# Second batch's head: tile 4 modulated between the moments, all row sums on VectorE, squares behind the copies of the transposes

## The chip, the cores and the metric

One core of a Trainium2 chip runs the whole program: two transformer layers on two sequences of 512 rows of 512 values. The metric is the device time of one execution in microseconds (us), lower being better. The core has five engines which each run their own queue strictly in order and meet through semaphores: TensorE (PE in the rows; its weight loads are PEld), VectorE (DVE), ScalarE (ACT), GpSimd (POOL) and SyncE (SP), which issues transfers.

## The reference, cut to what matters

The change touches only the step between the second layer's attention and its last block, for the second sequence. There the reference computes, row by row (512 values in a row):

```
h = _layernorm(x) * (1 + cb) + sb              # per row: (x - mean) / sqrt(var + 1e-5), then scaled and shifted
x_norm = h * rsqrt(mean(h * h) + RMS_EPS)
H_res_logits  = (x_norm @ W_res.T).reshape(B, T, 4, 4) + H_res_base
H_pre_logits  = x_norm @ W_pre.T + H_pre_base
H_post_logits = x_norm @ W_post.T + H_post_base
H_res = sinkhorn_log(H_res_logits)             # 50 alternating normalisations of every row's 4x4 matrix
...
return x + gb * (x_mixed + y_distributed)
```

`cb` and `sb` depend on the sequence alone. The three logits are 24 numbers per row. The 50 Sinkhorn iterations need the 16 `H_res` logits of the rows, and the kernel runs them for all 1024 rows at once.

## The kernel before, in words

The rows are held in 8 tiles of 128 rows by 512 values; tiles 0 to 3 are the first sequence, 4 to 7 the second. `acc[:, i, :]` is tile i of x, `hh[i // 4][:, i % 4, :]` the same tile of h. Each stage of a tile is a method of one name in each engine's class (`Vector`, `Scalar`, `Tensor`, `Pool`, `Sync`), and the story function calls them in one order; an engine that has nothing to do in a stage skips it. So the order of the calls is the order of every engine's queue. Nothing is planned at run time: the order is written by hand, and a wait at the front of a queue holds everything behind it on that engine.

The stages of one tile i of a head, the lines being those of the profile:

- `moments`: VectorE takes statistics of the row (L1114, L1116) and makes the negative mean and the variance plus epsilon (L1118, L1119); GpSimd makes the reciprocal root (L1773) and its product with the mean (L1775).
- `norm`: ScalarE writes the normalised row to `hh` (L1491).
- `scaled_rows`: VectorE multiplies by 1 + cb (L1126, in place); sb is then added in place either by GpSimd (L1783) or, for tiles 5 and 7, by VectorE (L1130). `h_rows_at(i)` names the semaphore of whoever adds, and the readers of the finished rows wait for it.
- `square`: ScalarE sums the squares of the row (L1606: the activation and a read of its accumulator).
- `turn_l`: TensorE transposes the tile's four 128x128 blocks (L800), and ScalarE copies them from PSUM to `hT4` (L1614).
- `rms`: VectorE scales the sum of squares (L1244), after waiting for ScalarE's square of this tile, and GpSimd takes the power -1/2 (L1857).
- `logits`: TensorE multiplies `hT4` by the 24 columns (L811, eight instructions per tile), and VectorE scales the result by the reciprocal root and adds the bias (L1250), after waiting for both.

For the first sequence the head is interleaved with the attention (`head(E, 0)`). For the second it stands alone in `last_head`, since the attention's last group has to be finished first (`residual_last`, L1105 and L1107). Before the change its order is: moments and norm of tiles 4 to 7; scaled rows of 4 to 7; then per tile `square`, `turn_l`, `rms`, and the `logits` of the tile before. The three waits of VectorE that matter below are these:

```
ve.wait_ge(*a_n("h", i))          # scaled_rows: this tile's norm on ScalarE
ve.wait_ge(*a_ss(i))              # rms: this tile's sum of squares on ScalarE
ve.wait_ge(*p_lg("l", i))         # logits: this tile's product on TensorE
```

Behind the head VectorE starts the Sinkhorn chain (`sk_scale`, L1256, which waits for the logits of tile 7), a chain of small dependent operations of VectorE up to `H` (L1304); beside it the other engines make the branch of the block. Then `finish` mixes the streams and writes the eight output tiles.

Of the kernel before, what the change touches and what calls it, by code (L numbers as in the profile page):

```python
# [69 lines left out]
def build(nc, I, out, cst_w):  # L70
# [3 lines left out]
    def sig(name, step=1):  # L74
        return Sig(ctx.enter_context(nc.semaphore(name)), step)
# [150 lines left out]
    for b in range(2):  # L226
# [53 lines left out]
    v_fw, v_fT, v_res, v_ln, v_hl, v_ffn, v_aw, v_qkv, v_part, v_pt, v_nm, v_mx, v_out = [sig(n) for n in  # L280
        ("v_fw", "v_fT", "v_res", "v_ln", "v_hl", "v_ffn", "v_aw", "v_qkv", "v_part", "v_pt", "v_nm", "v_mx", "v_out")]
# [8 lines left out]
    g_x, g_ln, g_vp, g_rot, g_mix, g_rr, g_pre = [sig(n) for n in ("g_x", "g_ln", "g_vp", "g_rot", "g_mix", "g_rr", "g_pre")]  # L290
# [58 lines left out]

    def h_rows_at(i):  # L350

        return v_ln("h", "d", i) if i in (5, 7) else g_ln("h", i)

    def most(t):

# [116 lines left out]
    class Tensor(Stages):  # L472
# [322 lines left out]
        def turn_l(self, i, bk):  # L795
            pe = self.e
            pe.wait_ge(*h_rows_at(i))
            pe.wait_ge(*self.drain[bk])
            for k in range(4):
                mm = pe.transpose(banks[bk][:, k * 128:(k + 1) * 128], hh[i // 4][:, i % 4, k * 128:(k + 1) * 128], ident)  # L800
            mm.then_inc(*p_lg.up("T", i))
            self.drain[bk] = a_hc(i)
# [32 lines left out]
    class Vector(Stages):  # L835
# [285 lines left out]
        def scaled_rows(self, i):  # L1121
            ve, b = self.e, i // 4
            h_ = hh[b][:, i % 4, :]
            ve.wait_ge(*a_n("h", i))
            ve.wait_ge(*d_mt[4, b](1))
            ve.tensor_tensor(h_, h_, mt[1, 4, b][:, :], ALU.mult).then_inc(*v_ln.up("h", "c", i))  # L1126
            if i in (5, 7):
                ve.wait_ge(*v_ln("h", "c", i))
                ve.wait_ge(*d_mt[3, b](1))
                ve.tensor_tensor(h_, h_, mt[1, 3, b][:, :], ALU.add).then_inc(*v_ln.up("h", "d", i))  # L1130
# [210 lines left out]
    class Scalar(Stages):  # L1341
# [259 lines left out]
        def square(self, i):  # L1601
            ac = self.e
            ac.wait_ge(*h_rows_at(i))
            if i:
                ac.wait_ge(*a_ss(i - 1))
            ac.activation(junk[:, :], hh[i // 4][:, i % 4, :], ACTF.Square,  # L1606
                          accum_out=fs["ss"][:, i:i + 1]).then_inc(*a_ss.up(i))
# [70 lines left out]
    class Pool(Stages):  # L1678
# [96 lines left out]
            po.tensor_tensor(nmr[:, i:i + 1], nmean[:, i:i + 1], rs[:, i:i + 1], ALU.mult).then_inc(*g_rr.up(of, i))  # L1775

        def scaled_rows(self, i):
            if i in (5, 7):
                return
            po, b, h_ = self.e, i // 4, hh[i // 4][:, i % 4, :]  # L1780
            po.wait_ge(*v_ln("h", "c", i))
            po.wait_ge(*d_mt[3, b](1))
            po.tensor_tensor(h_, h_, mt[1, 3, b][:, :], ALU.add).then_inc(*g_ln.up("h", i))  # L1783
# [594 lines left out]

    def last_head(E):

        E.residual_last(1)
        for i in range(4, 8):
            E.moments("h", i), E.norm("h", i)
        for i in range(4, 8):
            E.scaled_rows(i)
        for i in range(4, 8):
            E.square(i)
            E.turn_l(i, E.spin())
            E.rms(i)
            if i > 4:  # L2390
                E.logits(i - 1, E.spin())
        E.logits(7, E.spin())

    class Sink:
# [207 lines left out]
    def story(E):  # L2602
        layer0_head(E)
        layer0_loop(E)
        middle(E)
        line = stream(E, pass_a_line)
        parts(E, 0, line)
        parts(E, 1, line)
        pending = joined(stream(E, head, 0), stream(E, mixes, 0))
        attentions(E, line, pending)  # L2610
        pending.rest()
        last_head(E)
        merged(stream(E, first_half), stream(E, branch, 0)).rest()
        merged(stream(E, second_half), stream(E, branch, 1)).rest()
        stream(E, finish).rest()
        E.end()
# [87 lines left out]
```

## Time and profile before

| what | us |
|---|---|
| median of 3 runs | 1483.64 |
| lowest, highest run | 1483.23, 1487.5 |
| the profiled execution's own time | 1483.97 |
| its span, first to last instruction | 1481.5 |
| VectorE busy in the span | 1007.2 (68%) |
| TensorE busy in the span | 1230.3 (83%) |
| ScalarE busy in the span | 622.5 (42%) |
| GpSimd busy in the span | 737.1 (50%) |

The shares are averages over very different stages. The stretch that the change touches is some 18 us long, from 1314.6 (the first statistics of tile 4) to 1332.2 (the first Sinkhorn operation), and it is read by itself. In a timeline each line is one instruction or some alike in a row: start in us from the span's start, duration in us, engine, line, operation, output and input tiles with their shapes, count; in brackets the idle time of the engine ahead of it and what ended it. The duration of a line with xN runs from the first one's start to the last one's end.

### The profile page before, as it was taken

How to read it: one execution, taken by the hardware profiler on the slowest of the kernel's cores; microseconds unless marked ns; L12 is line 12 of the kernel's file. 1: busy time of each engine (PE TensorE's matmuls, PEld its weight loads, DVE VectorE, ACT ScalarE, POOL GpSimd, SP SyncE). 2: the span in 40 equal slices, each digit the busy share in tenths (PEclk: the TensorE clock that was granted, in tenths of full speed). 3: DMA queues.
4: the chain of work that ended last, by engine and by line, in shares of the span. 5: the costliest groups of instructions: out<-in, count | busy, mean ns of one | idle time of the engine just before them, and what ended most of it. 6: DMA issues, size and time to landing. Idle time of an engine off the chain costs nothing. (4 is left out here: it accounts for less than half of the span.)

```text
span 1481.5 us, 18424 instructions
## 1 busy us (share of the span) xinstructions
PE 1230.3 (83%) x6008; PEld 867.2 (59%) x6008; DVE 1007.2 (68%) x1721; ACT 622.5 (42%) x1166; POOL 737.1 (50%) x740
## 2 busy tenths in 40 slices
PE   4889999999999999999999999988979988961100
PEld 2578767776776776876776777766743333430000
DVE  5845665656655656665666656597778898659898
ACT  2334333433433433433433343338327777753303
POOL 0465756656755675576665675698410012031107
PEclk9899999999999999999999999999969999975555
DMA  4211122123122212222212111140485310000001
GB/s 163 79 52 59 45 77 72 58 57 89 54 72 72 63 45 72 58 57 65 64 44 78 54 47 57 51 137 7 91 152 81 52 48 2 1 1 0 0 0 57
DMA packets 70487, 86.45 MB, mean 58 GB/s; under 512 B 6789, under 2 KB 40741, under 8 KB 69818
## 3 DMA queue, kind: packets, MB, share of 16 engines
q1 hardware_dynamic: 68138, 81.52, 20.2%
q10 hardware_dynamic: 2256, 3.77, 0.9%
q8 instruction: 49, 0.80, 0.2%
q14 instruction: 44, 0.36, 0.1%
HBM read 77.49 MB, written 7.51 MB: 57 GB/s over the span
## 5 line engine op out<-in xcount | busy, mean ns | idle before, releaser
L1695 POOL TENSOR_TENSOR sw<-sw,sinT 128x512 f32<-128x512 f32 x80 | 103.3, 1291 | 138.9 <-ACT sw L1425 138.9
L1474 ACT ACTIVATE yTh<-yF 128x512 fp32r<-128x512 f32 x64 | 40.4, 632 | 308.1 <-DVE yF L1043 308.1
L1208 DVE TENSOR_REDUCE nm<-banks 128x2 f32<-128x1024 f32 x128 | 151.3, 1219 | 26.0 <-PE banks L750 25.9
L1709 POOL TENSOR_TENSOR dec<-gb,gcol 128x512 f32<-128x512 f32 x64 | 70.3, 1099 | 190.7 <-DVE Sd L1009 187.6
L1587 ACT ACTIVATE Pb<-banks 128x512 f32<-128x512 f32 x256 | 135.0, 601 | 47.6 <-PE banks L771 47.2
L981 DVE SCALAR_TENSOR_TENSOR gs<-tg,banks 128x512 f32<-128x512 f32 x64 | 44.0, 688 | 117.6 <-ACT tg L1432 117.6
L547 PE MATMUL banks<-hTh,wgh 128*128 128x512 f32 x256 | 122.2, 477 | 0.0
L599 PE MATMUL banks<-st,qt 128*128 128x128 f32 x384 | 78.8, 288 | 37.8 <-DVE Sd L1009 21.1
L625 PE MATMUL banks<-woh,yTh 128*128 128x512 f32 x256 | 104.8, 410 | 2.7 <-ACT yTh L1474 2.7
L547 PE MATMUL banks<-hTh,wqh 128*128 128x512 f32 x256 | 106.3, 415 | 0.0
L547 PE MATMUL banks<-hTh,wgl 128*128 128x512 f32 x256 | 101.0, 394 | 0.0
L547 PE MATMUL banks<-hTl,wgh 128*128 128x512 f32 x256 | 100.7, 393 | 0.0
L547 PE MATMUL banks<-hTh,wql 128*128 128x512 f32 x256 | 100.7, 393 | 0.0
L625 PE MATMUL banks<-wol,yTh 128*128 128x512 f32 x256 | 100.5, 393 | 0.0
L547 PE MATMUL banks<-hTl,wqh 128*128 128x512 f32 x256 | 99.9, 390 | 0.0
L1049 DVE TENSOR_TENSOR yTl<-yF,yTh 128x512 fp32r<-128x512 f32 x64 | 69.8, 1091 | 41.5 <-ACT yTh L1474 41.2
L771 PE MATMUL banks<-qsT,ksT 50*128 50x512 f32 x256 | 90.2, 487 | 8.2 <-DVE hh L1232 6.1
L600 PE MATMUL banks<-xc,Sd 128*128 128x128 f32 x512 | 94.1, 282 | 0.3 <-DVE Sd L1009 0.3
L976 DVE TENSOR_TENSOR tt<-banks,cosT 128x512 f32<-128x512 f32 x80 | 55.3, 691 | 52.7 <-ACT sw L1425 51.9
L1700 POOL TENSOR_TENSOR qT<-tt,sw 128x512 f32<-128x512 f32 x64 | 83.9, 1310 | 14.6 <-DVE tt L976 6.5
L599 PEld LDWEIGHTS banks<-st,qt 128*128 128x128 f32 x384 | 63.3, 200 | 47.0 <-DVE Sd L1009 25.3
L1432 ACT ACTIVATE tg<-banks 128x512 f32<-128x512 f32 x64 | 38.3, 598 | 119.9 <-PE banks L547 119.9
(310 smaller groups left out, 3291.4 us busy)
## 6 DMA issues: line engine op xcount, KB each, us to landing
gb<-g_scr SPq DMA_DIRECT2D x64, 256.0 KB, 3.5
raw<-in_wmod SPq DMA_DIRECT2D x40, 256.0 KB, 2.7
raw<-in_wg SPq DMA_DIRECT2D x32, 256.0 KB, 2.7
raw<-in_wo SPq DMA_DIRECT2D x32, 256.0 KB, 2.9
raw<-in_wq SPq DMA_DIRECT2D x30, 256.0 KB, 2.7
qsT<-q_scr SPq DMA_DIRECT2D x22, 256.0 KB, 7.1
q_scr<-hl SPq DMA_DIRECT2D x28, 128.0 KB, 4.8
mt<-mods_scr SPq DMA_DIRECT2D x12, 256.0 KB, 4.5
```

The costliest lines, as they stand in the source:

```text
L547: mm = pe.matmul(banks[bk][:, :], w_[:, k, :], x_[:, k, b * 512:(b + 1) * 512], start=(c == 0), stop=(c == 11))
L599: pe.matmul(o, qt[:, h, :], st[:, h, :], start=True, stop=False)
L600: mm = pe.matmul(o, Sd[:, h, :], xc[:, h, :], start=(n == 0), stop=True)
L625: pe.matmul(banks[bO][:, :], yTh[:, h, :], w_[:, :], start=(h == 0 and n == 0), stop=False)
L771: pe.matmul(banks[bk], k_[64 * g:64 * g + 50, p // 4, kt * 128:(kt + 1) * 128], q_[64 * g:64 * g + 50, p % 8, :], start=True, stop=True).t ...
L976: ve.tensor_tensor(tt1[j][:, :], banks[bk][:, :], cosT[:, :], ALU.mult).then_inc(*v_cos.up(kind, t, n))
L1049: ve.tensor_tensor(yTl[:, :, :], yF[:, :, :], yTh[:, :, :].bitcast(F32), ALU.subtract).then_inc(*v_yl.up(s))
L1208: ve.tensor_reduce(nm[:, b, i, p:32:16], pairs[z_][:, :].rearrange("p (g t) -> p g t", g=2), AX.X, ALU.max, negate=True).then_inc(*v_nm.up ...
L1587: ac.activation(Pb[kt % 2][:, 2 * g + pr, :], banks[bk], ACTF.Exp, scale=0.25).then_inc(*a_exp.up(b, qd, kt, pr, g))
L1695: po.tensor_tensor(s_[:, :], s_[:, :], sinT[:, :], ALU.mult).then_inc(*g_rope.up("sin", kind, t, n))
L1700: po.tensor_tensor(dst, tt1[j][:, :], s_[:, :], ALU.add).then_inc(*g_rope.up("add", kind, t, n))
L1709: po.tensor_tensor(dec[:, :, :], gb[s % 2][:, :, :], bc(gcol[:, t % 2, heads(t), n], 2, 128), ALU.subtract).then_inc(*g_dec.up("sub", s))
```

## The change

Three edits. `h_rows_at` and the two `scaled_rows` make VectorE add sb for all four tiles of the second sequence (GpSimd adds for the first sequence alone). In `last_head` tile 4's scaled rows and its transposes with their copy come ahead of the moments and norm of tile 7. And the rest goes tile by tile: for tiles 5 to 7 the scaled rows, the transposes with their copy and the logits of the tile before, then the square and `rms`, so that a square stands behind the copy of its tile's transposes on ScalarE.

```
     def h_rows_at(i):
-        return v_ln("h", "d", i) if i in (5, 7) else g_ln("h", i)
+        return v_ln("h", "d", i) if i > 3 else g_ln("h", i)
...
-            if i in (5, 7):
+            if i > 3:
                 ve.wait_ge(*v_ln("h", "c", i))
                 ve.wait_ge(*d_mt[3, b](1))
                 ve.tensor_tensor(h_, h_, mt[1, 3, b][:, :], ALU.add).then_inc(*v_ln.up("h", "d", i))
...
         def scaled_rows(self, i):      # GpSimd
-            if i in (5, 7):
+            if i > 3:
                 return
...
     def last_head(E):
         E.residual_last(1)
+        for i in (4, 5, 6):
+            E.moments("h", i), E.norm("h", i)
+        E.scaled_rows(4)
+        E.turn_l(4, E.spin())
+        E.moments("h", 7), E.norm("h", 7)
         for i in range(4, 8):
-            E.moments("h", i), E.norm("h", i)
-        for i in range(4, 8):
-            E.scaled_rows(i)
-        for i in range(4, 8):
+            if i > 4:
+                E.scaled_rows(i)
+                E.turn_l(i, E.spin())
+                E.logits(i - 1, E.spin())
             E.square(i)
-            E.turn_l(i, E.spin())
             E.rms(i)
-            if i > 4:
-                E.logits(i - 1, E.spin())
         E.logits(7, E.spin())
```

## Rows read from the trace of the kernel before

**Rows 1.** Chain of waits that ended last: start us, duration us, what.
```profile
1319.51 0.69 DVE hh L1126
1320.22 1.27 POOL hh L1783
1321.53 1.97 PE banks L800 x8
```

**Rows 2.** Timeline of VectorE, from tile 4's statistics to Sinkhorn.
```profile
1314.63 0.69 DVE L1114 BATCH_NORM_STATS2 bst<-acc 128x6 f32<-128x512 f32 x1
...
1317.84 0.68 DVE L1114 BATCH_NORM_STATS2 bst<-acc 128x6 f32<-128x512 f32 x1
...
1318.85 0.14 DVE L1119 TENSOR_SCALAR ve<-mv 128x1 f32<-128x1 f32 x1
1318.91 1.28 DVE L1126 TENSOR_TENSOR hh<-hh,mt 128x512 f32<-128x512 f32 x2
1320.23 1.80 DVE L1130 TENSOR_TENSOR hh<-hh,mt 128x512 f32<-128x512 f32 x1
1321.95 1.28 DVE L1126 TENSOR_TENSOR hh<-hh,mt 128x512 f32<-128x512 f32 x2
...
1327.72 0.24 DVE L1250 SCALAR_TENSOR_TENSOR lg<-banks,r,rbc 128x24 f32<-128x24 f32 x1 [1.72 <-PE banks L811]
1327.88 0.14 DVE L1244 TENSOR_SCALAR ss<-ss 128x1 f32<-128x1 f32 x1
...
1331.88 0.24 DVE L1250 SCALAR_TENSOR_TENSOR lg<-banks,r,rbc 128x24 f32<-128x24 f32 x1 [1.46 <-PE banks L811]
1332.16 0.23 DVE L1256 TENSOR_SCALAR W<-lg 128x128 f32<-128x128 f32 x1
```

**Rows 3.** Timeline of GpSimd in the same stretch.
```profile
1318.00 0.55 POOL L1773 TENSOR_TENSOR rs<-ve,neghalf 128x1 f32<-128x1 f32 x1 [0.25 <-DVE ve L1119]
...
1319.07 0.93 POOL L1773 TENSOR_TENSOR rs<-ve,neghalf 128x1 f32<-128x1 f32 x1 [0.25 <-DVE ve L1119]
...
1320.22 1.26 POOL L1783 TENSOR_TENSOR hh<-hh,mt 128x512 f32<-128x512 f32 x1
```

**Rows 4.** Timeline of ScalarE in the same stretch.
```profile
1316.72 0.81 ACT L1491 ACTIVATE hh<-acc,nmr,rs 128x512 f32<-128x512 f32 x1 [4.57 <-POOL nmr L1775]
...
1322.68 0.60 ACT L1614 ACTIVATE hT<-banks 128x512 f32<-128x512 f32 x1 [0.45 <-PE banks L800]
1323.18 0.62 ACT L1606 ACTIVATE junk<-hh 128x512 f32<-128x512 f32 x1
...
1323.69 0.19 ACT L1606 ACTIVATION_READ_ACCUMULATOR junk<-hh 128x1 f32 x1
```

**Rows 5.** Timeline of TensorE in the same stretch.
```profile
1312.20 0.66 PE L791 MATMUL banks<-cst,oS 128*128 128x128 f32 x4 [0.72 <-ACT oS L1594]
...
1325.06 1.09 PE L800 MATMUL banks<-cst,hh 128*128 128x128 f32 x4
1325.94 1.74 PE L811 MATMUL banks<-rwt,hT 128*128 128x24 f32 x8
...
1328.40 3.45 PE L811 MATMUL banks<-rwt,hT 128*128 128x24 f32 x16
```

**Rows 6.** Windows: busy us (count) of PE, PEld, DVE, ACT, POOL; PEclk; DMA.
```profile
1316.00:1316.50 0.50, 0.00 (x0) 0.00 (x0) 0.47 (x2) 0.00 (x0) 0.42 (x2) 0.65 0.00 0
...
1324.00:1328.00 4.00, 4.00 (x21) 4.00 (x22) 1.61 (x7) 2.31 (x6) 1.94 (x4) 0.50 0.00 0
...
1332.20:1389.00 56.80, 3.92 (x12) 2.51 (x12) 51.40 (x158) 13.60 (x45) 4.72 (x8) 0.50 0.00 0
```

**Rows 7.** Timeline of TensorE in the first sequence's head.
```profile
1244.39 0.66 PE L800 MATMUL banks<-cst,hh 128*128 128x128 f32 x4
...
1248.68 1.04 PE L811 MATMUL banks<-rwt,hT 128*128 128x24 f32 x8
```

**Rows 8.** Groups of one line, VectorE's product with 1 + cb, whole span.
```profile
L1126 DVE TENSOR_TENSOR hh<-hh,mt x8: 678/680/855, 1230.2 to 1322.5; 128x512 f32<-128x512 f32 x8
```

## The prediction, made before the changed kernel was run

> **What bounds the kernel now.** I read the page first and saw no engine that bounds the whole (TensorE 83%, VectorE 68%), so the stretch of the change has to be read alone. The chain of waits comes next, cut to that stretch [rows 1]: tile 4's statistics and its product with 1 + cb on VectorE, then GpSimd's sum of tile 4 (1.27 us at 1320.22), then TensorE, whose first eight transposes (tiles 4 and 5) start at 1321.53 and whose last sixteen products (tiles 6 and 7) end at 1331.85 [rows 5]. So the head now has two parts: up to 1321.53 the first tile is waited for, and from there on TensorE is the bound, with 4.00 us busy of 4.00 in 1324 to 1328 at a granted clock of 0.50, the 1.2 GHz level [rows 6]. Everything else (VectorE's sums, the squares, the copies) is done ahead of TensorE's need. The timelines of VectorE, ScalarE, GpSimd and TensorE of the same stretch [rows 2 to 5] give the prices. Behind the head VectorE is the bound: it is busy 51.40 us of 56.80 in the first half of Sinkhorn [rows 6], which starts 0.28 us after the last logits at 1331.88 [rows 2]. A shift of these last logits therefore goes to the end of the program one for one. The output tiles stand behind Sinkhorn and move with it.
>
> I call VectorE's product of tile i ci and its sum di, the transposes Ti, TensorE's products li, VectorE's logits gi.
>
> **Part 1, what is gained: tile 4 comes earlier.** c4 takes the place of tile 7's statistics at 1317.84 [rows 2]; norm 4 was done at 1316.72 + 0.81 = 1317.53 [rows 4], so nothing holds it. c4 takes 0.68 (median of eight [rows 8]), d4 follows after 0.04 (the gap between c5's end at 1320.19 and the sum at 1320.23 [rows 2]). A VectorE sum with GpSimd quiet is not in the trace. Bounds: 0.68, the product of the same shape, and 1.80, the sum beside GpSimd's [rows 2]. I take 0.68, because GpSimd has no wide operation left in this stretch. So d4 ends at 1317.84 + 0.68 + 0.04 + 0.68 = 1319.24, and T4 starts at 1319.29 (0.05 is the gap from GpSimd's end at 1321.48 to T4 at 1321.53 [rows 1, 3]): 2.24 us earlier than now.
>
> **Part 2, what is lost: VectorE's queue becomes a loop through all engines.** Now its queue is c4, c5, d5, c6, c7, d7, ss4, ss5, g4, ss6, g5, ss7, g6, g7 (ss is the small operation of `rms`). After the change it is c4, d4, moments 7, ss4, c5, d5, g4, ss5, c6, d6, g5, ss6, c7, d7, g6, ss7, g7. Two waits now stand in front of work that TensorE needs: ss4 waits for square 4 with c5 behind it, and g4 waits for l4, with c6 behind it; likewise g5 ahead of c7. And l4 stands behind T5 in TensorE's queue (both orders are T4, T5, l4, T6, l5, T7, l6, l7). So T6 can't start before g4, nor T7 before g5, where now T6 and T7 follow without a gap.
>
> First c5. Statistics of tile 7 start at 1319.16 (d4's end less an overlap of 0.08, as between the sum's end at 1322.03 and 1321.95 [rows 2]). From a tile's statistics to its norm it is 1316.72 - 1314.63 = 2.09 us [rows 2, 4], so norm 7 starts at 1321.25. Copy 4 is ahead of it on ScalarE and costs nothing: it starts at T4 + 1.15 = 1320.44 (1322.68 against 1321.53 [rows 1, 4]) and is over at 1321.04. Square 4 stands behind norm 7: the start of an activation behind another is some 0.1 before the other's end (0.50 pitch of a 0.60 copy [rows 4]), so 1321.25 + 0.72 = 1321.97. From a square's start to the end of its accumulator read it is 1323.88 - 1323.18 = 0.70 [rows 4]: 1322.67. With 0.06 for the wait, ss4 starts at 1322.73 and c5 0.07 later at 1322.80 (pitch of a one-column operation and the next: 1318.85 to 1318.91 [rows 2]). c5 ran at 1319.51 before [rows 1], so it is 3.29 us later.
>
> Then one turn of the loop, from c5 to c6:
> - c and d: 0.68 + 0.04 + 0.68 = 1.40
> - d's end to the transposes: 0.05
> - transposes to the start of the products behind them in the queue: 1325.94 - 1325.06 = 0.88 [rows 5]
> - products to g: 1327.72 - 1325.94 = 1.78 [rows 2, 5]
> - g to ss of the next tile 0.16 (1327.88 - 1327.72 [rows 2]), and 0.07 to c: 0.23
>
> The turn is 4.34 us. The squares don't lengthen it: copy 5 starts 1.13 after T5, square 5 0.5 later and is read 0.70 after that, 2.33 after T5, while g4 comes 2.66 after T5. Before, TensorE needed 0.88 + 3.45 / 2 = 2.61 us per tile [rows 5].
>
> c5 at 1322.80, c6 at 1327.14, c7 at 1331.48. Then 1.40 + 0.05 + 0.88 to l6, and from l6 to g7 3.48 (1331.88 - 1328.40 [rows 2, 5]), as l7 follows l6 without a gap: 5.81. So g7 is at 1337.29, against 1331.88.
>
> **Sum:** +5.41 us. The profiled execution's own 1483.97 becomes 1489.4. The median of the three runs is 0.33 below the profiled execution, so on it I forecast 1483.64 + 5.4 = 1489.0, slower by 0.36%.
>
> **Edits taken at nothing.** GpSimd loses its two sums (tile 4's took 1.26 us [rows 3]), and VectorE's sums lose the collision that makes tile 5's 1.80 us [rows 2]: two more short sums against two that get shorter leave VectorE about as much to do, and the waits between bound it. TensorE gets gaps; its clock is at 0.50 already (it fell in 1316.0 to 1316.5, 0.65 on average there, after the last matmul had ended at 1312.86 [rows 5, 6]), so it has no lower level to fall to. SyncE, the DMAs and the banks' order are untouched.
>
> **GpSimd beside c4.** The reciprocal root of tile 6 (1318.00 [rows 3]) will now run beside c4. That of tile 7, which started inside c4 of before, took 0.93 instead of 0.55, and the product c5 behind c4 kept its 0.68 [rows 2, 3]. So I charge nothing to VectorE; norm 6 is late by 0.4 us, and is not waited for before c6. The Trainium skill ("SBUF — State Buffer", section "Who interferes with whom") says that a VectorE instruction with two SBUF inputs contends with a GpSimd instruction reading SBUF and that the later one blocks fully until the earlier ends. The row bears this out for GpSimd's wait. By the rule alone d4, issued while the root of tile 6 runs, would be blocked in turn to about 1319.07, which moves d4, moments 7, norm 7, square 4 and c5 by 0.5 us: the sum would be +5.9 instead of +5.4. The row on c5 speaks for +5.4.
>
> **The bounds.** c and d six times at 0.855, the longest of the eight products [rows 8], are +1.05 for tiles 5 to 7; the waits between engines, ten at 0.04 to 0.1, may be off by 0.3 either way. If a lone sum cost 1.80 after all, the three sums in the path add 3.4. Likeliest case alone: +4.8 to +6.6, 1488.4 to 1490.2.
>
> **Rivals.**
> 1. The early tile carries through (faster). If c5 to c7 weren't held, T4 at 1319.29 would let TensorE run its 10.3 us from there and g7 would come 2.24 us earlier: 1481.4. It decides on one point: ss4 and g4 would have to find their waits met when VectorE comes to them. For it: TensorE is the bound from T4 on [rows 1]. Against it: ss4 would be ready only if square 4 were done at 1320.3, and it stands behind norm 7, which can't start before 1321.2; g4 needs T5, which needs c5.
> 2. TensorE's clock comes up, same within measurement. In the first sequence's head, at full clock, four transposes take 0.66 and eight products 1.04 [rows 7], where here it is 1.09 and 1.74 [rows 5]. With 0.60 for 0.88 and 1.08 for 1.78 the turn is 3.36, g7 at 1322.80 + 6.72 + 1.40 + 0.05 + 0.60 + 2.08 = 1333.65: +1.8, 1485.4. Against it: even 4.00 busy of 4.00 left the clock at 0.50 [rows 6], and the new order is less dense. The Trainium skill ("TensorE: Matmul & The Clock Gate", section "What's actually happening") says that a busy array is granted the full clock; the row at 4.00 busy disagrees for these small matmuls, so the rule gets little.
> 3. More than I charge: the sums collide after all (with the power of `rms` on GpSimd, which starts beside c5 to c7), each up to 1.1 us longer: +6.6 to +8.8, 1490.3 to 1492.5.
> 4. Part of the loop is shorter than I charge (a wait is put in the queue otherwise than I read it, or part of the shift is taken up in Sinkhorn's 5.4 us of idle time of VectorE [rows 6]): +2 to +4.4, 1485.6 to 1488.0. Against it: VectorE's gaps there are waits inside its own chain, which move along.
>
> **Chances.** Forecast 0.70, rival 1 0.04, rival 2 0.05, rival 3 0.09, rival 4 0.12. A measurement of this kernel tells a change from none at about 0.3%, 4.45 us. The forecast lies 0.95 us beyond that bound, with its own lower end of +4.8 still beyond it; I give a tenth of it to the other side for the medians' scatter. Slower: 0.63 + 0.09 = 0.72. Faster by more than 0.3% would need 4.45 us, twice what rival 1 gives: 0.02. Same: 0.26. The range of 1486.0 to 1491.5 takes in the forecast, the upper part of rival 4 and the lower of rival 3.
>
> **What the changed profile would show.** T4 near 1319.3; VectorE's c5 near 1322.8 with an idle time ended by ScalarE's square; VectorE idle some 2.7 us ahead of g4 and of g5, ended by TensorE's products; TensorE's transposes of tiles 5, 6 and 7 each after an idle time ended by VectorE, 4.3 us apart; the lone sums at 0.68; clock 0.50; the last logits near 1337.3. If T6 follows T5 within 3 us, or if c5 stands ahead of 1321, the loop isn't there and the forecast is wrong. If the sums take over 1 us, rival 3 holds.

## The result, and the profile after

The changed kernel takes 1489.6 us (median of 22 runs, 1485.06 to 1494.76), the kernel before 1484.2 us (median of 22 runs, 1480.56 to 1491.28): a difference of 5.4 us and a ratio of 1.0035, with a 95% interval of 1.0025 to 1.0045. The forecast was +5.4 us.

The two profiled executions differ in the stretch of the change and hardly elsewhere. I measure that stretch as H: from the start of tile 4's statistics to the start of tile 7's logits on VectorE. It was 1331.88 - 1314.63 = 17.25 us [rows 2] and is now 1336.32 - 1313.57 = 22.75 us, 5.50 more. What comes behind it, to the end of the span, was 149.62 us and is 149.68. What comes ahead was 1.06 us shorter in this execution, which the change doesn't touch; that is why the spans (1481.5 and 1486.0) differ by 4.5 only. The profiled execution's own time is 1488.98.

The timeline after, VectorE's lines and two of GpSimd's that fall beside them, cut to those that answer to [rows 2] (columns as there):

```profile
1313.57 0.69 DVE L1114 BATCH_NORM_STATS2 bst<-acc 128x6 f32<-128x512 f32 x1
...
1316.77 0.68 DVE L1126 TENSOR_TENSOR hh<-hh,mt 128x512 f32<-128x512 f32 x1
1316.93 0.93 POOL L1773 TENSOR_TENSOR rs<-ve,neghalf 128x1 f32<-128x1 f32 x1 [0.25 <-DVE ve L1119]
1317.49 0.69 DVE L1130 TENSOR_TENSOR hh<-hh,mt 128x512 f32<-128x512 f32 x1
...
1321.64 0.15 DVE L1244 TENSOR_SCALAR ss<-ss 128x1 f32<-128x1 f32 x1 [2.39 <-ACT junk L1606]
1321.72 0.69 DVE L1126 TENSOR_TENSOR hh<-hh,mt 128x512 f32<-128x512 f32 x1
...
1325.88 0.24 DVE L1250 SCALAR_TENSOR_TENSOR lg<-banks,r,rbc 128x24 f32<-128x24 f32 x1 [2.74 <-PE banks L811]
1326.04 0.14 DVE L1244 TENSOR_SCALAR ss<-ss 128x1 f32<-128x1 f32 x1
1326.10 0.68 DVE L1126 TENSOR_TENSOR hh<-hh,mt 128x512 f32<-128x512 f32 x1
1326.26 0.93 POOL L1857 TENSOR_TENSOR r<-ss,neghalf 128x1 f32<-128x1 f32 x1 [3.44 <-DVE ss L1244]
1326.82 0.69 DVE L1130 TENSOR_TENSOR hh<-hh,mt 128x512 f32<-128x512 f32 x1
...
1330.47 0.68 DVE L1126 TENSOR_TENSOR hh<-hh,mt 128x512 f32<-128x512 f32 x1
...
1336.32 0.24 DVE L1250 SCALAR_TENSOR_TENSOR lg<-banks,r,rbc 128x24 f32<-128x24 f32 x1 [1.40 <-PE banks L811]
```

VectorE now stands idle three times with a tile's rows behind the wait: 2.39 us for square 4, ahead of c5, and 2.74 us each for the products of tiles 4 and 5, ahead of c6 and c7 (a third such wait, ahead of the logits of tile 6, holds no rows). TensorE's timeline shows the other half of the loop, where [rows 5] had no idle time:

```profile
1318.23 1.12 PE L800 MATMUL banks<-cst,hh 128*128 128x128 f32 x4 [6.43 <-DVE hh L1130]
1323.19 1.12 PE L800 MATMUL banks<-cst,hh 128*128 128x128 f32 x4 [3.84 <-DVE hh L1130]
1324.10 1.74 PE L811 MATMUL banks<-rwt,hT 128*128 128x24 f32 x8
1327.56 1.11 PE L800 MATMUL banks<-cst,hh 128*128 128x128 f32 x4 [1.72 <-DVE hh L1130]
1328.47 1.74 PE L811 MATMUL banks<-rwt,hT 128*128 128x24 f32 x8
1331.93 1.11 PE L800 MATMUL banks<-cst,hh 128*128 128x128 f32 x4 [1.72 <-DVE hh L1130]
1332.84 3.45 PE L811 MATMUL banks<-rwt,hT 128*128 128x24 f32 x16
```

The transposes of tiles 5 to 7 each wait for VectorE's sum. The windows of the changed kernel show what that does to TensorE; the first answers to the window 1324 to 1328 of [rows 6], where it was busy for all 4.00 us:

```profile
1324.00:1328.00 4.00, 2.28 (x12) 2.16 (x11) 1.59 (x4) 1.21 (x3) 0.93 (x1) 0.50 0.00 0
1328.00:1332.00 4.00, 2.28 (x13) 2.16 (x12) 1.59 (x4) 1.21 (x3) 0.93 (x1) 0.50 0.00 0
```

And the chain of waits of the changed kernel (start us, duration us, what) goes through three engines where [rows 1] had stayed on TensorE:

```profile
1320.90 0.71 ACT junk L1606 x2
1321.64 0.04 DVE ss L1244
...
1321.72 0.70 DVE hh L1126
...
1322.45 0.70 DVE hh L1130
...
1323.19 1.12 PE banks L800 x4
1324.31 1.55 PE banks L811 x8
```

### The profile page after: what moved, and what is told of

It is laid out like the page before. It is cut to its first block and busy times, and to the rows that moved or that the text cites. A ratio compares the mean times of both kernels' runs of the same rounds, so it can differ in the third digit from the quotient of the medians.

```text
span 1486.0 us, 18424 instructions
## 1 busy us (share of the span) xinstructions
PE 1232.9 (83%) x6008; PEld 869.7 (59%) x6008; DVE 1006.2 (68%) x1723; ACT 622.8 (42%) x1166; POOL 736.8 (50%) x738
```

## The experiments

The theory: the loss is the order of VectorE's queue alone, since two waits (ss4 for ScalarE's square; g4 and g5 for TensorE's products) stand ahead of rows that TensorE needs. The main rivals: the sums moved to VectorE are what costs, or tile 4's place between the moments. The kernels below are written with one list of stages per engine, so that one engine's queue can be changed by itself: m is moments and norm, s the scaled rows, T the transposes with their copy, q the square, r the rms, l the logits, each with its tile. In VectorE's queue s is what the prediction calls c and d, r is ss and l is g. The changed kernel's list is `m4 m5 m6 s4 T4 m7 q4 r4 s5 T5 l4 q5 r5 s6 T6 l5 q6 r6 s7 T7 l6 q7 r7 l7`. A ratio of times is uncertain by 0.1 to 0.2% either way and many effects are no larger, so the verdicts rest on H, which is read from one profiled execution of each kernel, with the ratio of the times beside it. Two things speak for H: where two kernels have the same waits it agrees (22.75 and 22.76 for the changed kernel and e8), and in every row the interval of the ratio takes in what the difference in H alone would make of the time.

| kernel | H, us | against before | expected H | ratio of times, 95% interval |
|---|---|---|---|---|
| before | 17.25 | | | |
| changed | 22.75 | +5.50 | 22.7 | 1.0035 (1.0025 to 1.0045) |
| e1_sums_only | 16.37 | -0.88 | 16.7 | 0.9987 (0.9968 to 1.0005) |
| e2_no_loop | 16.36 | -0.89 | 16.7 | 0.9989 (0.9975 to 1.0004) |
| e3_loop_alone | 24.89 | +7.64 | 24.9 | 1.0046 (1.0030 to 1.0063) |
| e4_square_wait_out | 20.08 | +2.83 | 20.0 | 1.0018 (1.0002 to 1.0034) |
| e5_logits_wait_out | 22.13 | +4.88 | 22.1 | 1.0047 (1.0031 to 1.0062) |
| e6_two_tiles_early | 16.24 | -1.01 | 15.3 to 15.6 | 1.0004 (0.9991 to 1.0017) |
| e7_two_tiles_warm | 16.24 | -1.01 | 13.0 | 0.9991 (0.9978 to 1.0003) |
| e8_after_warm | 22.76 | +5.51 | 19.0 or 22.7 | 1.0039 (1.0024 to 1.0053) |
| e9_free_bank | 15.30 | -1.95 | 15.3 | 0.9989 (0.9974 to 1.0004) |
| e10_free_bank_warm | 13.57 | -3.68 | 13.4 | 0.9977 (0.9961 to 0.9993) |

### The sums alone

```
 (kernel before, with i > 3 for i in (5, 7) in the three places; last_head as before)
```

> The kernel before with one part of the change: VectorE adds sb for tiles 4 and 6 too; the order stays. H is the head's length, from the start of tile 4's statistics to the start of tile 7's logits on VectorE (17.25 us before, 22.75 us after). Loop theory (the change's loss is all in the order of VectorE's queue, the sums moved are a small gain): T4 can start 5.74 into H, T5 is the bound at 7.05, and from there TensorE needs 0.9 + 3 x 2.61 less one step: H about 16.7, 0.5 us less than before, time of before within measurement. Rival (VectorE is dearer with all sums, and the loss is there): H above 17.3, up to 22.

Its timeline, the rows of tile 4 on VectorE and the first transposes:

```profile
1319.41 0.68 DVE L1126 TENSOR_TENSOR hh<-hh,mt 128x512 f32<-128x512 f32 x1
1320.12 0.69 DVE L1130 TENSOR_TENSOR hh<-hh,mt 128x512 f32<-128x512 f32 x1
...
1320.87 1.11 PE L800 MATMUL banks<-cst,hh 128*128 128x128 f32 x4 [7.51 <-DVE hh L1130]
...
1322.20 1.12 PE L800 MATMUL banks<-cst,hh 128*128 128x128 f32 x4 [0.22 <-DVE hh L1130]
```

H is 1331.50 - 1315.13 = 16.37: the sums on VectorE are a gain of 0.88 us. The time is the same within its interval. The rival that blamed them falls. A lone sum takes 0.69 us, against 1.80 beside GpSimd's [rows 2].

### The change without the loop

```
-VectorE: m4 m5 m6 s4 m7 r4 s5 l4 r5 s6 l5 r6 s7 l6 r7 l7
+VectorE: m4 m5 m6 s4 m7 s5 s6 s7 r4 r5 l4 r6 l5 r7 l6 l7
```

> The changed kernel with VectorE's queue alone reordered: c4, d4, moments 7, c5, d5, c6, d6, c7, d7, and only then the small operations of rms and the logits. All else as in the change, tile 4 early included. Loop theory: H about 16.7 (T4 at 4.66, but T5 at 7.05 since c5 stands behind the moments of tile 7; from T5 on 9.6 us as now), 6.1 us less than the changed kernel and 0.5 less than before; the early tile by itself earns nothing. Rival (the early tile carries through when nothing holds it): H 15.0, 2.2 us less than before. Rival (the waits are not the cause): H stays at 22.7.

```profile
1318.90 1.12 PE L800 MATMUL banks<-cst,hh 128*128 128x128 f32 x4 [6.44 <-DVE hh L1130]
...
1321.29 1.11 PE L800 MATMUL banks<-cst,hh 128*128 128x128 f32 x4 [1.28 <-DVE hh L1130]
...
1322.20 1.74 PE L811 MATMUL banks<-rwt,hT 128*128 128x24 f32 x8
```

H is 1330.59 - 1314.23 = 16.36: reordering VectorE's queue alone takes back 6.39 us and leaves a kernel 0.89 us shorter here than before. TensorE's queue, ScalarE's and GpSimd's are those of the change, so VectorE's order is enough to take the loss away. It need not be the only cure: that l4 stands behind T5 in TensorE's queue is part of the loop too, and no run moved it. The rows say a second thing: T4 starts 4.67 into H and then T5 waits 1.28 us for VectorE, at 7.06 into H. In e1, with tile 4 behind all moments, T5 starts at 7.07. So T5 is what starts the dense part, and moving tile 4 alone ahead of the moments of tile 7 earns 0.01 us.

### The loop alone

```
 (kernel before: GpSimd adds sb for tiles 4 and 6)
-all: m4 m5 m6 m7 s4 s5 s6 s7 q4 T4 r4 q5 T5 r5 l4 q6 T6 r6 l5 q7 T7 r7 l6 l7
+all: m4 m5 m6 m7 s4 T4 q4 r4 s5 T5 l4 q5 r5 s6 T6 l5 q6 r6 s7 T7 l6 q7 r7 l7
```

> The kernel before (GpSimd adds sb for tiles 4 and 6, all moments first) with the tile by tile order of the change alone: scaled rows, transposes, logits of the tile before, square and rms, tile by tile. Loop theory: c5 waits for square 4 and c6, c7 for the logits of two tiles before; with GpSimd's sum and its power standing in the loop of tile 6 too, H about 24.9, 7.6 us more than before, time slower by 0.5%. Rival (the order costs nothing, what costs is the sums on VectorE or tile 4's place between the moments): H 17.3.

H is 1339.91 - 1315.02 = 24.89, and the time is higher by 0.46% (0.30 to 0.63): the tile by tile order by itself costs 7.64 us. In the full change the other two edits hide 2.14 us of that (24.89 to 22.75). The theory gave 24.9. VectorE's waits ahead of c5, c6 and c7:

```profile
1324.32 0.15 DVE L1244 TENSOR_SCALAR ss<-ss 128x1 f32<-128x1 f32 x1 [4.33 <-ACT junk L1606]
...
1328.56 0.24 DVE L1250 SCALAR_TENSOR_TENSOR lg<-banks,r,rbc 128x24 f32<-128x24 f32 x1 [2.75 <-PE banks L811]
...
1333.84 0.24 DVE L1250 SCALAR_TENSOR_TENSOR lg<-banks,r,rbc 128x24 f32<-128x24 f32 x1 [4.38 <-PE banks L811]
```

The last one is longer because GpSimd's power for tile 5 and its sum of tile 6 stand in that turn.

### One wait out at a time

```
 e4  VectorE: m4 m5 m6 s4 m7 s5 r4 l4 s6 r5 l5 s7 r6 l6 r7 l7
 e5  VectorE: m4 m5 m6 s4 m7 r4 s5 r5 s6 r6 s7 l4 l5 r7 l6 l7
```

> The changed kernel with one of the two waits taken from the front of VectorE's scaled rows: the small operation of rms (which waits for the square) stands behind the scaled rows of the next tile; the logits still stand ahead of the scaled rows of the tile after next. Loop theory: c5 starts at 5.6 instead of 8.15 into H and the turn is 4.30 instead of 4.37, so H about 20.0, 2.7 us less than the changed kernel. If the waits were independent costs of equal size, the turn would fall too, by up to 2.4 us each: H 15 to 16. If the square's wait is no cost: H 22.7.

> The changed kernel with the other wait taken from the front of VectorE's scaled rows: logits of tiles 4 and 5 stand behind the scaled rows of tile 7, while the small operation of rms still stands ahead of the next tile's scaled rows. Loop theory: c5 stays at 8.15 into H, the turn is closed by the square instead (1.40 + 0.05 + 2.33 to the read of the sum + 0.15 = 3.94 instead of 4.37), and T7 waits for its bank, which the logits of tile 4 free behind d7: H about 22.1, 0.6 us less than the changed kernel. The two waits then overlap: taken out one by one they give 2.7 and 0.6 us, together 6.4. If the logits' wait were the cost by itself, H would fall to 17 to 18 here.

Without the square's wait H is 20.08, 2.67 less than the changed kernel; without the logits' wait 22.13, 0.62 less; without both (e2) 6.39 less. The waits overlap: of these 6.39 us the logits' wait alone keeps 3.72 (e4) and the square's alone 5.77 (e5). What e4 takes back is nearly all ahead of the loop, since T5 starts at 7.07 instead of 9.62; its turn is 4.31 us. In e5 0.25 us of H is another wait: T7 starts 0.30 us after d7 instead of 0.05, once the logits of tile 4 have freed its bank (more on that below). VectorE's rows of e5 show the loop closed by the square instead:

```profile
1323.81 0.69 DVE L1126 TENSOR_TENSOR hh<-hh,mt 128x512 f32<-128x512 f32 x1
...
1327.67 0.15 DVE L1244 TENSOR_SCALAR ss<-ss 128x1 f32<-128x1 f32 x1 [2.44 <-ACT junk L1606]
1327.75 0.69 DVE L1126 TENSOR_TENSOR hh<-hh,mt 128x512 f32<-128x512 f32 x1
```

A turn is 3.94 us there against 4.38 in the changed kernel. That a square stands behind its tile's copy costs nothing where no rows stand behind the wait for it (e2 has that order and e1 has not: 16.36 and 16.37). That it lengthens e5's turn is read from ScalarE's queue; no run with the squares ahead of the copies shows it.

### Both of the first tiles early

```
 VectorE: m4 m5 m6 s4 s5 m7 s6 s7 r4 r5 l4 r6 l5 r7 l6 l7
 ScalarE: m4 m5 m6 T4 q4 T5 m7 q5 T6 q6 T7 q7
```

> The order without the loop, and tile 5's scaled rows too ahead of the moments of tile 7 (on ScalarE the copies and the square of tiles 4 and 5 stand around tile 7's norm as they come due). Theory (T5 is what bounds the start of TensorE's block, not T4): T5 at 5.98 into H, H about 15.3 to 15.6, 1.0 us less than with tile 4 alone early, 1.7 to 2.0 less than before, time lower by 0.13%. Rival (tile 7 becomes late, its moments being pushed back by 1.3 us): T7 is late and H stays at 16.4.

H is 1331.61 - 1315.37 = 16.24, only 0.12 less than with tile 4 alone early: a miss. T5 did start at 6.00, as expected, but the rows near the end show a gap that I had not foreseen:

```profile
1324.64 0.69 DVE L1126 TENSOR_TENSOR hh<-hh,mt 128x512 f32<-128x512 f32 x1 [0.93 <-ACT hh L1491]
...
1325.36 0.69 DVE L1130 TENSOR_TENSOR hh<-hh,mt 128x512 f32<-128x512 f32 x1
...
1326.85 0.24 DVE L1250 SCALAR_TENSOR_TENSOR lg<-banks,r,rbc 128x24 f32<-128x24 f32 x1 [0.67 <-POOL r L1857]
...
1327.24 1.09 PE L800 MATMUL banks<-cst,hh 128*128 128x128 f32 x4 [0.76 <-DVE ss L1244]
```

Tile 7's rows are done at 1326.05, but T7 starts at 1327.24. Its PSUM bank is the one of tile 4's products (three banks go round), which VectorE's logits of tile 4 free; these stood behind d7. T7 starts 0.15 us after they end, at 1327.09, though the bracket names the `ss` behind them. That the bank is the cause needs a run:

```
-VectorE: m4 m5 m6 s4 s5 m7 s6 s7 r4 r5 l4 r6 l5 r7 l6 l7
+VectorE: m4 m5 m6 s4 s5 m7 s6 r4 l4 s7 r5 r6 l5 r7 l6 l7
```

> As the version with two tiles early, with VectorE's logits of tile 4 moved ahead of the scaled rows of tile 7, into the 0.93 us in which VectorE waits for tile 7's norm. There T7 stood 0.76 us behind a wait for VectorE: its PSUM bank is freed by the logits of tile 4. Theory (the missing 0.9 us of that version was the bank): T7 follows l5 at once, H about 15.3, 0.9 less than that version, 1.9 less than before, time lower by 0.13%. Rival (T7 was late because of its rows, that is of tile 7's late moments): H stays at 16.2.

H is 1331.94 - 1316.64 = 15.30, as the bank theory had it; T7 follows l5 without idle time:

```profile
1326.00 1.74 PE L811 MATMUL banks<-rwt,hT 128*128 128x24 f32 x8
...
1327.56 1.09 PE L800 MATMUL banks<-cst,hh 128*128 128x128 f32 x4
...
1328.13 0.24 DVE L1250 SCALAR_TENSOR_TENSOR lg<-banks,r,rbc 128x24 f32<-128x24 f32 x1 [0.37 <-POOL r L1857]
1328.45 3.45 PE L811 MATMUL banks<-rwt,hT 128*128 128x24 f32 x16
```

Logits of tile 4 ahead of tile 6's rows are one of the waits of the changed kernel's loop; ahead of tile 7's rows they cost nothing here, since VectorE would have waited for tile 7's norm at that point anyway. In time, e9 is not told apart from before (0.9989, interval to 1.0004).

### The clock

```
+def warm(self, n):                      # TensorE; nothing reads banks[0] here
+    for _ in range(n):
+        self.e.transpose(banks[0][:, 0:128], ident, ident)
 e7   two tiles early, e8   the changed kernel:  warm(40) behind the attention's last transposes
 e10  e9 with warm(54) there, warm(9) between T4 and T5, warm(5) ahead of T6 and of T7
```

> As the version with two tiles early, and 40 transposes of the identity into a bank that nobody reads are queued on TensorE behind the attention's last ones, over its idle time ahead of the head. Theory (the head is bound by TensorE at the 1.2 GHz level): with the clock kept at 1.00 four transposes take 0.6 and eight products 1.04 instead of 0.9 and 1.73; H about 13.0, bounded by VectorE's scaled rows of tile 7 (d7 ends at 10.2 into H), 4.3 us less than before, time lower by 0.3%. Rivals: the clock falls in the head all the same (H 15.3 as without), or the filler isn't done when tile 4 is ready (H above 15.3).

> The changed kernel with the same 40 filler transposes and nothing else. If the clock stays up through the loop's gaps (TensorE is busy 1.6 us of a turn), the turn is 3.4 instead of 4.37 and H about 19.0, still 1.8 us more than before: the loop costs at either clock. If the clock falls again once the filler ends: H 22.7 as in the changed kernel, with the first transposes alone at the higher level.

> As the version with the free bank, with 54 filler transposes of the identity ahead of T4, 9 between T4 and T5, 5 ahead of T6 and 5 ahead of T7, into a bank that nobody reads. Theory (the clock fell at 1321.4 in the version with 40 fillers because TensorE stood idle from 1316.7 to 1318.8 and in pieces after it): with the gaps filled the clock stays at 1.00, H about 13.4, 3.9 us less than before, time lower by 0.26%. Rival (these transposes and products of 24 columns don't hold the clock however dense they stand): the clock falls some 4 to 5 us after the long filler's end, and H is 15.3 or, with the fillers in the way at the lower level, up to 17.

The 40 fillers did not help: H of e7 is 1330.36 - 1314.12 = 16.24, that of e8 1337.66 - 1314.90 = 22.76, both unchanged. For e7 there are two reasons, and its expected 13.0 left out the first: T7 starts 11.87 into H in e6 and in e7 alike, as it waits for the bank behind d7, so the faster matmuls ahead of it could earn nothing. Behind it the clock was down again. In e8, T4 ran at the 2.4 GHz level and T5, after 4.30 us of idle time, at 1.2 GHz:

```profile
1319.58 0.65 PE L804 MATMUL banks<-cst,hh 128*128 128x128 f32 x4 [2.08 <-DVE hh L1134]
...
1324.53 1.12 PE L804 MATMUL banks<-cst,hh 128*128 128x128 f32 x4 [4.30 <-DVE hh L1134]
```

In e7 the granted clock held at 1.00 to 1321 and fell in the next microsecond although TensorE had work at that time (windows: PE, PEld, DVE, ACT, POOL busy; PEclk):

```profile
1317.00:1318.00 1.00, 0.00 (x0) 0.00 (x0) 0.96 (x4) 0.75 (x2) 0.70 (x2) 1.00 0.00 0
...
1320.00:1321.00 1.00, 0.88 (x9) 0.88 (x9) 0.93 (x5) 0.91 (x4) 0.00 (x0) 1.00 0.02 8
1321.00:1322.00 1.00, 0.84 (x6) 0.71 (x5) 0.96 (x4) 0.41 (x1) 0.79 (x1) 0.58 0.00 0
```

With more fillers ahead and the gaps filled as well (e10) the clock stayed at 1.00 through the whole head:

```profile
1316.00:1320.00 4.00, 3.45 (x32) 3.23 (x30) 3.85 (x9) 2.56 (x6) 1.49 (x3) 1.00 0.03 6
1320.00:1321.00 1.00, 0.75 (x8) 0.52 (x6) 0.49 (x2) 0.49 (x1) 0.83 (x3) 1.00 0.00 0
...
1324.00:1325.00 1.00, 1.00 (x11) 1.00 (x10) 0.23 (x2) 1.00 (x4) 0.00 (x0) 1.00 0.00 0
```

Sixteen products take 1.92 us there instead of 3.45 [rows 5], H is 1325.66 - 1312.09 = 13.57, and the time is 0.9977 of before (0.9961 to 0.9993): 1481.66 us, median of 12, against 1485.68 on the same chip. So this version is faster than before by 0.23%, and its H is 9.18 us shorter than the changed kernel's. Against e9 H is 1.73 us shorter, and 1.56 of that stand behind T7's start (2.82 us to the last logits instead of 4.38); T7 itself, which waits for tile 7's rows, comes only 0.17 earlier. The last logits wait for GpSimd's power, no longer for TensorE, whose products end at 1325.26:

```profile
1325.66 0.24 DVE L1254 SCALAR_TENSOR_TENSOR lg<-banks,r,rbc 128x24 f32<-128x24 f32 x1 [0.56 <-POOL r L1861]
```

## Why the prediction was right

The steps, counted from the start of tile 4's statistics:

| step | predicted | measured |
|---|---|---|
| T4 starts | 4.66 | 4.66 |
| a lone sum on VectorE | 0.68 | 0.69 |
| c5 starts, behind square 4 | 8.17 | 8.15 |
| a turn of the loop, c5 to c6 | 4.34 | 4.38 |
| c7 to g7 | 5.81 | 5.85 |
| H | 22.66 | 22.75 |

**Part 1, the early tile,** came as far as T4. That it would earn nothing even without the loop was not in the prediction: rival 1 let TensorE run its 10.3 us from T4 on and priced the freed order at -2.24 us. The runs give it -0.89, because c5 stands behind the moments of tile 7 and T5 can't start before 7.06 (e1 and e2). The rival failed where I said it would, at its waits, but its price was also too high.

**Part 2, the loop,** is shown by four runs: it comes alone with the order (e3), goes with VectorE's queue (e2), and goes in parts with each wait (e4, e5). That the squares don't lengthen a turn held too: with the logits' wait gone the turn falls by 0.44 us to what the square allows.

**Edits taken at nothing.** GpSimd's reciprocal root beside c4 took 0.93 us, as the row on tile 7's had it, and d4 behind it kept 0.69. So VectorE was not blocked in turn, and the 0.5 us that the Trainium skill's rule ("SBUF — State Buffer", "Who interferes with whom") would have added by the reading in the prediction did not come. Rival 3 falls with it: beside VectorE's rows it is GpSimd's power of `rms` that takes 0.93 to 0.95 instead of 0.55, and nobody waits for it there.

**The bounds** were not added up rightly, which did no harm. By the prediction's own terms (0.3 either way, 1.05 up) the likeliest case runs from +5.1 to +6.8, not from +4.8 to +6.6. And a dear sum would count four times, not three, since d4 stands ahead of the moments of tile 7: +4.5 us instead of +3.4. The lone sums took 0.69.

**Rival 2, the clock.** It did not come up by itself. Its conditional price, +1.8 us for the changed order at full clock, was never measured, as in e8 the clock fell before T5.

**Downstream** the shift went through one for one (149.62 and 149.68 us behind the last logits), so rival 4's absorption in Sinkhorn did not occur.

What stays open: the start of the head differs between profiled executions by up to 6 us (1312.09 in e10, 1318.05 in e4), more than the change moves. But for the fillers of e7, e8 and e10 all kernels are alike ahead of that point; no run was made to find out what differs there. It makes single times of this kernel useless for effects of this size. Open too is why the clock of the kernel before stays down while TensorE is busy.

## What to carry to other kernels

When work is reordered tile by tile, write down the queue of every engine and look at what stands behind each wait: a small result that nobody needs soon (here a sum of squares and 24 logits) must not stand ahead of rows that the bounding engine needs next. Moving one tile forward earned 0.01 us here (e1 to e2); moving the next one too earned 1.06 (e2 to e9), but only once the bank that is handed round was emptied in time, a wait that the order of the rows doesn't show. Read such a change by one stretch of the trace, not by the time.

## What the runs showed of the hardware

- TensorE at the 1.2 GHz level did not come back up in the kernel before, though it was busy for 4.00 us of 4.00 [rows 6]. The Trainium skill ("TensorE: Matmul & The Clock Gate", "What's actually happening") has a busy array granted the full clock; this stretch of transposes and 24-column products, busy by the trace's busy time, disagrees. With fillers from the start and in the gaps the clock stayed at 1.00 through the head (e10); no run shows whether the head's own work would hold it there.
- A filler transpose of 128x128 takes 0.11 us (54 in 6.06 us). As TensorE was idle there, they delayed nothing: T4 starts 4.67 into H in e10 and in e2 alike. The nine between T4 and T5 made T5 0.15 us later than in e9 (6.14 and 5.99), and no wait behind it grew by that: T7 was waiting for tile 7's rows.
- Of VectorE's 128x512 product or sum and GpSimd's one-column power, only the latter gets longer when they meet (0.55 to 0.93 us). Of two 128x512 operations that start together VectorE's took 1.80 us [rows 2] against 0.69 alone.
